# Gated attention and two expert layers on one core: routing with one division, the first second-stage expert's splits and slot loads elsewhere, the last rows by tile

## The chip, the cores and the metric

The kernel runs on one core of a Trainium2 chip. The metric is the device time of one execution in microseconds (us). The core has a matmul engine (TensorE, PE in the profile, with its weight loads as PEld), VectorE (DVE), ScalarE (ACT), GpSimd (POOL) and SyncE (SP), which only issues DMAs here. Each engine runs its own list of instructions in order, and they meet at semaphores.

## What is computed

The input is 16 sequences of 128 tokens with 256 features. Four residual blocks follow each other: attention with 16 heads over a context, a soft mixture of eight experts with silu gates, attention with one head, and a switch layer in which each token goes to one of eight experts that has 256 places. The parts that the change touches:

```python
def _routing_weights(x, Wr, temperature):                 # block 2
    inh = sigmoid(x @ Wr / temperature)
    in_zone = (inh >= GOLDEN_LOWER) & (inh <= GOLDEN_UPPER)
    dist = abs(inh - GOLDEN_CENTER)
    w = exp(-dist / 0.1) * in_zone
    no_expert = w.sum(-1, keepdims=True) < 1e-08
    fb = exp(-dist / 0.3)
    fb_w = fb * (one_hot(top_k(fb, 2)).sum(-2))
    fb_w = fb_w / clip(fb_w.sum(-1, keepdims=True), 1e-08)
    w = where(no_expert, fb_w, w)
    return w / clip(w.sum(-1, keepdims=True), 1e-08)

# block 4: di = the tokens of each expert, in the order of their places
h = relu(einsum('ecm,emh->ech', di, w1)); eo = einsum('ech,ehm->ecm', h, w2)
out = x + tanh(g_ffn[1]) * (gate of the token * its row of eo)
```

## The kernel before

Float32 products are made of three matmuls: each operand is split into a high part (a rounded copy) and a low part (the value less the copy), and high*high, high*low and low*high are summed in PSUM. So each weight matrix that is loaded needs a high half, which ScalarE writes, and a low half, a subtraction by VectorE or GpSimd.

*First stage.* A loop written out in Python goes over the 16 sequences (`b`), with attention of one sequence and the eight experts (`gate_up`, `down`) of an earlier group of four sequences between its pieces. The routing weights of a group are made by VectorE at four places: `zones`, `two_best` and `expert_weights` (L1138) in the step after the group's last sequence, for groups 0 to 2, and once more after the loop for group 3. Each routing instruction goes through `seq`, which waits for it before the next. `expert_weights` writes `w_exp`, and `accumulate` (L1070) behind it adds the first expert's result with it to `x_all`. TensorE's next `down` half waits for that on the semaphore `ac`, as PSUM has one bank for both halves.

*Second attention.* From about 550 us on, `turn3(ga, gb)` runs on each engine: it finishes group `gb` and begins group `ga`. The last call is `turn3(None, 3)`. In it VectorE normalises the rows (`root_b`, whose steps are L262 to L267, and `normalise_b`), makes the low half of their transposes (`xb_low`), and after TensorE's gate logits picks the expert and the place of each token (`pick_expert`, `count_experts`, `pick_place`). GpSimd then sends the group's rows to their places in a buffer `slots` in HBM with four indirect DMAs (`dispatch`, L2224). ScalarE's list in that turn: `probs_copy`, `split(0, 0, 0)` (the high half of the first expert's w1, L746), `xb_high` (L787), `logits1_copy`, `gate_exp`; `split(0, 0, 1)` for w2 comes behind the turn. The low half of w1 is `split_w1(0, 0)` on GpSimd (L2214), between the dispatches of groups 2 and 3; that of w2 is `split_w2(0, 0)` on VectorE (L1541), behind the turn.

*Second stage.* When all rows are dispatched, SyncE loads slots (`xs`, one row of 260 floats for each of 2048 places, 16 tiles) and the next expert's weights (`load4`). An expert takes half a turn: `slots_norm` (VectorE, L1531), `slots_transposed` (TensorE), high and low half of the transposes, eight `hidden` blocks in four PSUM banks (TensorE L1591, ScalarE's `relu` L880, VectorE's low half L1545), `down4` (TensorE L2097), `rows_out` (VectorE L1553 and L1556: row numbers, then one update for each of the two tiles) and `scatter` (GpSimd L2245: two indirect DMAs to the output). The next expert's slots and weight halves are made in the same half-turn. Three turns of two experts run in a loop on the device, the fourth is written out. `alone` is a `sem_inc` between waits.

Of the kernel before, what the change touches and what calls it, by code (L numbers as in the profile page):

```python
# [8 lines left out]
ALU = mybir.AluOpType  # L9
# [7 lines left out]
P = 128  # L17
# [81 lines left out]
def block_kernel(nc, x, ctxT, maskf, mask0, gx, gf, wa0, bcols, bv0, bo0, w0, wrs, temp, wa1, bv1,  # L99
                 w1, w2, const, out, slots, kept):  # L100
    with ExitStack() as ctx:
# [235 lines left out]
        s_xs = [sem("first_slots_loaded"), sem("other_slots_loaded")]  # L337
# [10 lines left out]
        s_sc = [sem(f"rows_scattered{i}") for i in range(2)]  # L348
        ds4 = Steps(sem("vector_step4"), 2)
# [51 lines left out]
        def _(sp):  # L401
# [132 lines left out]
            for n, tiles in enumerate((slice(0, 4), slice(4, B))):  # L534
                sp.dma_start(xs[:, tiles, :], slots[tiles.start * P:tiles.stop * P, :].rearrange("(t p) c -> p t c", p=P)
                             ).then_inc(s_xs[n], 16)
                if n == 0:
                    load4(1, slice(1, 2))
# [12 lines left out]
        def _(act):  # L551
# [294 lines left out]
            def turn3(ga, gb):  # L846

                probs_copy(gb)
                if ga is None:
                    act.wait_ge(a1, 2 * G)  # L850
                    split(0, 0, 0)
                else:
                    xa_high(ga)
                    k1_evict(ga)
                    q1_evict(ga)
# [37 lines left out]
            split(0, 0, 1)  # L893
# [6 lines left out]
        def _(dve):  # L900
# [201 lines left out]
            def divide_by_sum(i):  # L1102
                seq(dve.tensor_reduce(rs[2], r[i], AX.X, ALU.add))
                seq(dve.tensor_scalar(rs[2], rs[2], 1e-8, None, ALU.max))
                seq(dve.reciprocal(rs[2], rs[2]))
                seq(dve.tensor_tensor(r[i], r[i], over_e(rs[2]), ALU.mult))

# [30 lines left out]
            def expert_weights(g):  # L1138
                divide_by_sum(7)
                seq(dve.tensor_tensor(r[7], r[7], over_e(rs[1]), ALU.mult))  # L1140
                seq(dve.tensor_tensor(rt[4], rt[4], rt[7], ALU.add))
                divide_by_sum(4)
                if g >= 2:
                    dve.wait_ge(ac, 2 * E * (g - 1))
                dve.tensor_scalar(w_exp[g % 2], r[4], tgate[:, 2:3], None, ALU.mult).then_inc(s_wexp, 1)
# [349 lines left out]

            def turn3(ga, gb):
# [11 lines left out]
                if ga is not None:  # L1508
                    mask_and_max(ga)
# [13 lines left out]
            for s in (xd_ok, di_lo, w4_l2, h1_lo, y4, ds4, idx4):  # L1523
                s.credit(dve)

# [22 lines left out]
            def rows_out(g, i):  # L1548
                dve.wait_ge(d4.sem, d4.now(g, i + 1))
# [4 lines left out]
                for j in range(2):  # L1554
                    row = xs[:, t + j, :] if isinstance(g, int) else xs[:, bass.ds(t + j, 1), :].rearrange("p a c -> p (a c)")
                    ins = dve.scalar_tensor_tensor(yo[i][j], ps[:, 4 + i, j * D:(j + 1) * D], row[:, D + 2:D + 3],  # L1556
# [3 lines left out]
            def turn(g, last):  # L1560
                for i in range(2):
                    nxt = (g, 1) if i == 0 else (g + 1, 0)
                    more = i == 0 or not last
                    if more:
                        if i == 1:
                            dve.wait_ge(s_xs[1], 16)
                        slots_norm(*nxt)
                    for f in range(8):
                        hidden_low(g, i, f)
                    if more:  # L1570
                        slots_low(*nxt)
                        split_w2(*nxt)
                    rows_out(g, i)
            split_w2(0, 0)
# [8 lines left out]
        def _(pe):  # L1583
# [504 lines left out]
            def down4(g, i):  # L2088
                pe.wait_ge(w4_hi.sem, w4_hi.now(g, 2 * i + 2))
                pe.wait_ge(w4_l2.sem, w4_l2.now(g, i + 1))  # L2090
                pe.wait_ge(y4.sem, y4.before(g, i + 1))
                for j in range(2):
                    for f in range(8):
                        if j == 0:
                            pe.wait_ge(h1_lo.sem, h1_lo.now(g, 8 * i + f + 1))
                        for n, (a, b) in enumerate(THREE):
                            mm = pe.matmul(ps[:, 4 + i, j * D:(j + 1) * D], h4[i][a][:, f, j * P:(j + 1) * P],  # L2097
                                           w4[i][b][:, 1, f * D:(f + 1) * D], start=(f == 0 and n == 0), stop=(f == 7 and n == 2))
                mm.then_inc(d4.sem, 1)

            def turn(g, last):
                for i in range(2):
# [4 lines left out]
                    down4(g, i)  # L2107
# [6 lines left out]
        def _(pool):  # L2114
# [119 lines left out]
            split_w1(0, 0)  # L2234
# [3 lines left out]
            def scatter(g, i):  # L2238
                pool.wait_ge(y4.sem, y4.now(g, i + 1))
                pool.wait_ge(ds4.sem, ds4.now(g, i + 1))  # L2240
                pool.wait_ge(idx4.sem, idx4.now(g, i + 1))
                alone(pool)
                for j in range(2):

# [65 lines left out]
```

## Time and profile before

| | |
|---|---|
| median of 3 runs | 763.89 us (762.23 to 765.86) |
| profiled execution | 764.7 us |
| its span, first to last instruction | 762.9 us |
| mean granted TensorE clock | 0.921 |
| busy: PE / DVE / ACT / POOL | 646.4 / 521.0 / 331.2 / 229.1 us |
| first stage | to about 562 us |
| second attention | about 562 to 638 us |
| dispatch and load of the slots | about 638 to 650 us |
| second stage | about 650 to 762.9 us |

All views come from the profiled execution, and their times count from the start of its span. A line names the start, the duration, the engine, the source line, the operation, output and inputs with their shapes, and how many like instructions it merges. What stands in brackets is the time in which the engine sat idle just before, and what ended it. Matmul ends are modelled.

### The profile page before, as it was taken

Reading aid. Unit: us, or ns where it says so; the run is one execution under the profiler, and the core shown is the slowest. Engines: PE = TensorE matmul, PEld = TensorE weight load, DVE = VectorE, ACT = ScalarE, POOL = GpSimd, SP = SyncE. Lnnn points to the kernel's source line nnn. Section 1 sums busy time; section 2 is a strip of 40 time slices with the busy share of each in tenths; the row PEclk is TensorE's granted clock in tenths of the full one; section 3 lists DMA queues with packets and bytes.
Section 4 is the critical chain, followed back from the end, with each engine's and each line's share of the span. In section 5 each row is a group of like instructions: output and inputs, shape, how many; then the busy total and the mean of one; then the engine's idle time right before and its main releaser. Section 6 shows DMA issues by size and latency. Waiting matters only on the chain.

```text
span 762.9 us, 12648 instructions
## 1 busy us (share of the span) xinstructions
PE 646.4 (85%) x4564; PEld 546.7 (72%) x4564; DVE 521.0 (68%) x1362; ACT 331.2 (43%) x530; POOL 229.1 (30%) x155
## 2 busy tenths in 40 slices
PE   5978598899899899999799889999966931799995
PEld 4656366787678778778688777898855821799995
DVE  6877987677877866866776647479458883466662
ACT  4434155355356456456355325152523321455641
POOL 2444624566532212221014010010031242255542
PEclk9879779899999999999999999999989955799998
DMA  7303303335442242333243424434221141964700
GB/s 225 121 15 127 125 1 139 125 135 211 180 166 83 85 165 84 137 113 125 83 165 113 162 87 152 132 124 146 83 69 43 61 161 43 318 210 153 242 20 26
DMA packets 43463, 94.51 MB, mean 124 GB/s; under 512 B 3519, under 2 KB 24383, under 8 KB 42384
## 3 DMA queue, kind: packets, MB, share of 16 engines
q1 hardware_dynamic: 41344, 87.62, 33.6%
q0 software_dynamic: 2064, 6.16, 2.3%
q8 instruction: 33, 0.54, 0.3%
q14 instruction: 22, 0.18, 0.1%
HBM read 72.94 MB, written 21.04 MB: 123 GB/s over the span
## 4 chain that ended last, share of the span: by engine, by line
PE 65%; DVE 24%; issue 5%; ACT 2%; DMA 1%; POOL 1%; DVEq 0%; SPq 0%; ACTq 0%; POOLq 0%
PE psum L1591 43%; PE psum L2097 6%; PE psum L1668 2%; PE psum L1698 2%; PE psum L1628 2%; PE psum L1662 2%; DVE work L1063 1%; DVE scratch L266 1%; DVE x_all L1079 1%; PE psum L1635 1%; PE psum L1647 1%; DVE work L951 1%; PE psum L1962 1%; PE psum L1893 1%; PE psum L1945 1%
## 5 line engine op out<-in xcount | busy, mean ns | idle before, releaser
L1591 PE MATMUL psum<-arena 128*128 128x256 f32 (+1 forms) x2544 | 446.0, 334 | 33.8 <-DVE x_all L1079 15.6
L1591 PEld LDWEIGHTS psum<-arena 128*128 128x128 f32 x2544 | 384.5, 199 | 78.4 <-DVE x_all L1079 14.8
L2135 POOL TENSOR_TENSOR diag<-neg_ident,work 128x1024 fp32r<-128x1024 f32 x32 | 60.9, 1904 | 249.3 <-DVE work L1010 242.5
L1063 DVE TENSOR_TENSOR work<-work,psum 128x512 f32<-128x512 f32 x64 | 43.9, 686 | 62.1 <-PE psum L1591 57.3
L625 ACT ACTIVATE arena<-work 128x512 fp32r<-128x512 f32 x64 | 40.3, 630 | 90.7 <-DVE work L1063 78.7
L1079 DVE SCALAR_TENSOR_TENSOR x_all<-psum,w_exp,x_all 128x256 f32<-128x256 f32 x128 | 55.9, 479 | 27.7 <-PE psum L1591 26.9
L618 ACT ACTIVATE work<-psum 128x512 f32<-128x512 f32 x64 | 38.2, 597 | 56.8 <-PE psum L1591 56.3
L1068 DVE TENSOR_TENSOR arena<-work,arena 128x512 fp32r<-128x512 f32 x64 | 51.8, 810 | 8.7 <-ACT arena L625 8.2
L2218 POOL TENSOR_TENSOR arena<-work,arena 128x1024 fp32r<-128x1024 f32 x4 | 9.5, 2370 | 151.1 <-ACT arena L641 151.1
L1010 DVE TENSOR_REDUCE work<-psum 128x8 f32<-128x1024 f32 x32 | 39.0, 1220 | 15.7 <-PE psum L1647 15.6
L593 ACT ACTIVATE work<-psum 128x1024 f32<-128x1024 f32 x32 | 32.8, 1026 | 35.4 <-PE psum L1668 32.3
L2097 PE MATMUL psum<-arena 128*128 128x256 f32 x384 | 47.9, 284 | 0.0
L2097 PEld LDWEIGHTS psum<-arena 128*128 128x128 f32 x384 | 46.6, 192 | 0.0
L2214 POOL TENSOR_TENSOR arena<-work,arena 128x2048 fp32r<-128x2048 f32 x8 | 37.0, 4621 | 15.9 <-ACT arena L746 15.9
L880 ACT ACTIVATE arena<-psum 128x256 fp32r<-128x256 f32 x64 | 22.6, 385 | 44.1 <-PE psum L1591 43.5
L1545 DVE SCALAR_TENSOR_TENSOR arena<-psum,arena 128x256 fp32r<-128x256 f32 x64 | 24.9, 421 | 20.2 <-ACT arena L880 19.0
L618 ACT ACT_TABLE_LOAD x26 | 33.4, 1283 | 0.5
L746 ACT ACTIVATE arena<-work 128x2048 fp32r<-128x2048 f32 x16 | 30.5, 1907 | 5.1 <-DMA work<-in_w 5.1
L1662 PE MATMUL psum<-arena 32*128 32x256 f32 x384 | 32.6, 303 | 0.2 <-DVE arena L1003 0.2
L2245 POOL DMA_INDIRECT out<-work,out_idx x16 | 15.8, 990 | 51.0 <-DVE work L1556 48.5
L2224 POOL DMA_INDIRECT slots<-x_all,tok_idx x16 | 16.8, 1048 | 42.4 <-DVE tok_idx L1418 38.7
L1662 PEld LDWEIGHTS psum<-arena 32*128 32x128 f32 x384 | 25.9, 192 | 0.8 <-issue 0.8
(194 smaller groups left out, 844.8 us busy)
## 6 DMA issues: line engine op xcount, KB each, us to landing
arena<-kept SPq DMA_DIRECT2D x24, 1024.0 KB, 5.6
work<-in_w SPq DMA_DIRECT2D x16, 1024.0 KB
kept<-arena SPq DMA_DIRECT2D x8, 1536.0 KB, 6.1
arena<-kept SPq DMA_DIRECT2D x24, 512.0 KB, 4.8
work<-in_w SPq DMA_DIRECT2D x8, 768.0 KB, 7.8
slots<-fill POOLq DMA_DIRECT2D x1, 2080.0 KB
work<-in_ctxT SPq DMA_DIRECT2D x8, 256.0 KB, 3.0
work<-in_ctxT SPq DMA_DIRECT2D x4, 512.0 KB, 5.2
```

The source lines that it names most:

```text
L593: act.activation(probs[u % 2], ps[:, ST:ST + 2, :].rearrange("p j (h q) -> p (j h) q", q=P), ACT.Exp, scale=DH ** -0.5).then_inc(ex, 1)
L618: act.activation(gu[i % 2], ps[:, GA, :], ACT.Silu).then_inc(sl, 1)
L625: act.activation(hT[n % 2][0][:, m, :], gu[i % 2], ACT.Copy).then_inc(hh, 1)
L1010: dve.tensor_reduce(mx[u % 2], ps[:, MX:MX + 2, :].rearrange("p j (h k) -> p (j h) k", k=P), AX.X, ALU.max).then_inc(mx_ok, 1)
L1063: dve.tensor_tensor(gu[i % 2], gu[i % 2], ps[:, UP, :], ALU.mult).then_inc(hm, 1)
L1068: dve.tensor_tensor(hT[n % 2][1][:, m, :], gu[i % 2], hT[n % 2][0][:, m, :], ALU.subtract).then_inc(hl, 1)
L1079: ins = dve.scalar_tensor_tensor(x_all[:, g * GB + t, 0:D], ps[:, DN, j * D:(j + 1) * D], w_exp[g % 2][:, t, e:e + 1], x_all[:, g * GB + t ...
L1591: mm = pe.matmul(dst, left(i, k), right(j, k), start=(n == 0), stop=(n == 3 * K2 - 1))
L1662: pe.matmul(ps[:, ST + j, m * 256:(m + 1) * 256], kT[h % 2][i][r:r + 32, m, t:t + P], qM[h % 2][jj][r:r + 32, m, :, t:t + P], start=False, ...
L2097: mm = pe.matmul(ps[:, 4 + i, j * D:(j + 1) * D], h4[i][a][:, f, j * P:(j + 1) * P], w4[i][b][:, 1, f * D:(f + 1) * D], start=(f == 0 and ...
L2135: pool.tensor_tensor(diag, neg_ident[:, :].rearrange("p (o q) -> p o q", o=1).to_broadcast([P, 8, P]), mx[u % 2].rearrange("p (h o) -> p h ...
L2214: pool.tensor_tensor(w4[i][1][:, 0, :], raw4[i][:, 0, :], w4[i][0][:, 0, :], ALU.subtract).then_inc(w4_l1.sem, 1)
```

## The change

One division in the routing: the two best experts' weights are no longer divided by their own sum before they are chosen, the clips at 1e-8 go, and the last division becomes a factor in the instruction that writes `w_exp`. ScalarE makes both high halves of the first second-stage expert within the last attention turn. The w1 low half moves from GpSimd to VectorE, between `xb_low` and `pick_expert`; the w2 low half moves behind a wait for all dispatches. The first load of slots is cut into two of two tiles. In the second stage `slots_norm` moves from ahead of the eight low halves to behind the fourth. In the very last half-turn TensorE signals after the first tile and writes the second tile into bank 4, and VectorE updates tile by tile. In every half-turn GpSimd sends each tile once its own update is there.

```diff
-            s_xs = [sem("first_slots_loaded"), sem("other_slots_loaded")]
+            s_xs = [sem(f"{n}_slots_loaded") for n in ("first", "second", "other")]
+            d4_first = sem("last_out_first_tile_ready")
@@ SyncE
-            for n, tiles in enumerate((slice(0, 4), slice(4, B))):
+            for n, tiles in enumerate((slice(0, 2), slice(2, 4), slice(4, B))):
                 sp.dma_start(xs[:, tiles, :], slots[...]).then_inc(s_xs[n], 16)
-                if n == 0:
+                if n == 1:
                     load4(1, slice(1, 2))
@@ ScalarE, turn3
                 if ga is None:
                     act.wait_ge(a1, 2 * G)
                     split(0, 0, 0)
+                    split(0, 0, 1)
...
-            split(0, 0, 1)
             slots_high(0, 0)
@@ VectorE, routing
             def expert_weights(g):
-                divide_by_sum(7)
                 seq(dve.tensor_tensor(r[7], r[7], over_e(rs[1]), ALU.mult))
                 seq(dve.tensor_tensor(rt[4], rt[4], rt[7], ALU.add))
-                divide_by_sum(4)
+                seq(dve.tensor_reduce(rs[2], r[4], AX.X, ALU.add))
+                seq(dve.reciprocal(rs[2], rs[2]))
                 if g >= 2:
                     dve.wait_ge(ac, 2 * E * (g - 1))
-                dve.tensor_scalar(w_exp[g % 2], r[4], tgate[:, 2:3], None, ALU.mult).then_inc(s_wexp, 1)
+                dve.scalar_tensor_tensor(w_exp[g % 2], r[4], tgate[:, 2:3], over_e(rs[2]), ALU.mult, ALU.mult
+                                         ).then_inc(s_wexp, 1)
@@ VectorE, turn3
+            def first_split(a, done):
+                dve.wait_ge(w4_hi.sem, w4_hi.now(0, a + 1))
+                dve.tensor_tensor(w4[0][1][:, a, :], raw4[0][:, a, :], w4[0][0][:, a, :], ALU.subtract).then_inc(done, 1)
...
                 xb_low(gb)
-                if ga is not None:
+                if ga is None:
+                    first_split(0, w4_l1.sem)
+                else:
                     mask_and_max(ga)
...
+            dve.wait_ge(s_disp, 16 * B + 16)
+            first_split(1, w4_l2.sem)
@@ VectorE, second stage
-            def rows_out(g, i):
-                dve.wait_ge(d4.sem, d4.now(g, i + 1))
+            def rows_out(g, i, last):
+                if last:
+                    dve.wait_ge(d4_first, 1)
+                else:
+                    dve.wait_ge(d4.sem, d4.now(g, i + 1))
...
                 for j in range(2):
+                    if last and j:
+                        dve.wait_ge(d4.sem, d4.now(g, i + 1))
-                    ins = dve.scalar_tensor_tensor(yo[i][j], ps[:, 4 + i, j * D:(j + 1) * D], row[:, D + 2:D + 3],
+                    ins = dve.scalar_tensor_tensor(yo[i][j], ps[:, 4 if last and j else 4 + i, j * D:(j + 1) * D], row[:, D + 2:D + 3],
                                                    row[:, 0:D], ALU.mult, ALU.add)
...
-                    if more:
-                        if i == 1:
-                            dve.wait_ge(s_xs[1], 16)
-                        slots_norm(*nxt)
                     for f in range(8):
                         hidden_low(g, i, f)
+                        if more and f == 3:
+                            dve.wait_ge(s_xs[1 + i], 16)
+                            slots_norm(*nxt)
...
-            split_w2(0, 0)
@@ TensorE
-            def down4(g, i):
+            def down4(g, i, last):
...
+                if last:
+                    pe.wait_ge(y4.sem, y4.now(g, 1))
                 for j in range(2):
+                    bank = 4 if last and j else 4 + i
...
+                    if last and j == 0:
+                        mm.then_inc(d4_first, 1)
@@ GpSimd
-            split_w1(0, 0)
             dispatch(G - 1)
...
             def scatter(g, i):
-                pool.wait_ge(y4.sem, y4.now(g, i + 1))
-                pool.wait_ge(ds4.sem, ds4.now(g, i + 1))
                 pool.wait_ge(idx4.sem, idx4.now(g, i + 1))
                 alone(pool)
-                for j in range(2):
+                for j, rows in enumerate((ds4, y4)):
+                    pool.wait_ge(rows.sem, rows.now(g, i + 1))
+                    alone(pool)
                     pool.indirect_dma_start(...)
```

## Rows read from the trace of the kernel before

**Rows 1.** Page, chain that ended last: share of the span by engine.
```profile
PE 65%; DVE 24%; issue 5%; ACT 2%; DMA 1%; POOL 1%; DVEq 0%; SPq 0%; ACTq 0%; POOLq 0%
```

**Rows 2.** Timeline (start us, us, engine, line, operation, idle before), routing of group 0.
```profile
132.78 0.18 DVE L1103 TENSOR_REDUCE work<-work 128x4 f32<-128x32 f32 x1
...
133.64 0.19 DVE L1140 TENSOR_TENSOR work<-work 128x32 f32<-128x32 f32 x1
...
134.31 0.17 DVE L1104 TENSOR_SCALAR work<-work 128x4 f32<-128x4 f32 x1
...
134.73 0.19 DVE L1106 TENSOR_TENSOR work<-work 128x32 f32<-128x32 f32 x1
134.95 0.24 DVE L1145 TENSOR_SCALAR w_exp<-work,tgate 128x32 f32<-128x32 f32 x1
...
136.24 5.99 PE L1591 MATMUL psum<-arena 128*128 128x256 f32 x31 [2.88 <-DVE x_all L1079]
```

**Rows 3.** Timeline, TensorE behind the routing of group 1.
```profile
258.26 5.07 PE L1591 MATMUL psum<-arena 128*128 128x256 f32 x38 [2.59 <-DVE x_all L1079]
```

**Rows 4.** Timeline, last attention turn.
```profile
618.51 1.91 ACT L746 ACTIVATE arena<-work 128x2048 fp32r<-128x2048 f32 x1 [5.13 <-DMA work<-in_w]
...
620.51 4.49 POOL L2214 TENSOR_TENSOR arena<-work,arena 128x2048 fp32r<-128x2048 f32 x1 [1.51 <-ACT arena L746]
620.63 4.38 DVE L266 SCALAR_TENSOR_TENSOR scratch<-scratch,work 128x4 f32<-128x4 f32 x1
...
625.45 0.16 DVE L266 SCALAR_TENSOR_TENSOR scratch<-scratch,work 128x4 f32<-128x4 f32 x1
...
628.05 0.60 ACT L787 ACTIVATE arena<-psum 128x512 fp32r<-128x512 f32 x1 [7.63 <-PE psum L1893]
...
634.53 0.19 DVE L1390 TENSOR_REDUCE work<-psum 128x4 f32<-128x32 f32 x1 [4.30 <-PE psum L1980]
```

**Rows 5.** Timeline, dispatch of the last group.
```profile
638.77 2.29 DVE L1541 TENSOR_TENSOR arena<-work,arena 128x2048 fp32r<-128x2048 f32 x1 [0.55 <-issue]
639.79 2.11 POOL L2224 DMA_INDIRECT slots<-x_all,tok_idx  x1 [0.30 <-issue]
642.21 0.97 POOL L2224 DMA_INDIRECT slots<-x_all,tok_idx  x1 [0.30 <-issue]
```

**Rows 6.** Timeline, first slots; last, the 256 KB context loads (KB, us to landing).
```profile
646.11 0.37 SPq L535 DMA_DIRECT2D x_all<-slots  x1
...
649.89 0.74 DVE L1531 TENSOR_SCALAR work<-x_all 128x256 f32<-128x256 f32 x2 [8.83 <-DMA x_all<-slots]
...
656.84 1.90 ACT L746 ACTIVATE arena<-work 128x2048 fp32r<-128x2048 f32 x1
...
work<-in_ctxT SPq DMA_DIRECT2D x8, 256.0 KB, 3.0
```

**Rows 7.** Timeline, end of the kernel.
```profile
748.08 5.92 PE L2097 MATMUL psum<-arena 128*128 128x256 f32 x48
...
754.12 0.87 DVE L1556 SCALAR_TENSOR_TENSOR work<-psum,x_all 128x256 f32<-128x256 f32 x2
755.89 0.98 POOL L2245 DMA_INDIRECT out<-work,out_idx  x1 [9.23 <-DVE work L1556]
757.17 0.98 POOL L2245 DMA_INDIRECT out<-work,out_idx  x1 [0.30 <-issue]
```

**Rows 8.** Timeline, second expert's hidden blocks in the second stage.
```profile
672.43 1.42 DVE L1545 SCALAR_TENSOR_TENSOR arena<-psum,arena 128x256 fp32r<-128x256 f32 x4 [1.34 <-ACT arena L880]
672.90 1.49 PEld L1591 LDWEIGHTS psum<-arena 128*128 128x128 f32 x12 [0.33 <-DVE arena L1545]
...
674.34 0.46 PEld L2074 LDWEIGHTS psum<-cst,work 128*128 128x128 f32 x4
```

**Rows 9.** Windows: stretch, its length, busy us (count) by engine, PEclk, DMA share, GB/s.
```profile
134.00:140.60 6.60, 4.36 (x20) 4.36 (x21) 4.83 (x13) 0.63 (x1) 3.12 (x3) 0.50 0.00 0
...
478.90:482.10 3.20, 3.20 (x17) 3.20 (x17) 0.88 (x3) 0.56 (x1) 0.00 (x0) 0.50 0.00 0
650.70:659.30 8.60, 6.80 (x30) 6.40 (x31) 2.44 (x6) 3.62 (x6) 0.47 (x1) 0.50 1.08 363
```

More of the change, by code:

```diff
@@ L1100, in first_of_max @@
                 seq(dve.tensor_tensor(dst, dst, over_e(rs[3]), ALU.is_equal))
[L1102 to L1106, printed above, removed]
             def routing_z(g):
@@ L1572, in turn @@
                         split_w2(*nxt)
-                    rows_out(g, i)
-            split_w2(0, 0)
+                    rows_out(g, i, last and i == 1)
             dve.wait_ge(s_xs[0], 16)
@@ L2096, in down4 @@
                         for n, (a, b) in enumerate(THREE):
-                            mm = pe.matmul(ps[:, 4 + i, j * D:(j + 1) * D], h4[i][a][:, f, j * P:(j + 1) * P],
+                            mm = pe.matmul(ps[:, bank, j * D:(j + 1) * D], h4[i][a][:, f, j * P:(j + 1) * P],
                                            w4[i][b][:, 1, f * D:(f + 1) * D], start=(f == 0 and n == 0), stop=(f == 7 and n == 2))
+                    if last and j == 0:
+                        mm.then_inc(d4_first, 1)
                 mm.then_inc(d4.sem, 1)
@@ L2106, in turn @@
                         slots_transposed(*((g, 1) if i == 0 else (g + 1, 0)))
-                    down4(g, i)
+                    down4(g, i, last and i == 1)
             slots_transposed(0, 0)
```

## The prediction

> **What bounds the kernel now.** I read the chain of waits first. By its shares [rows 1] the chain is two thirds TensorE and one quarter VectorE, and the DMAs have 1%. So a VectorE step is worth something only where TensorE stands still for it, and the timeline has to say where that is. Around the edits there are five such places. (a) In each of the four routing groups TensorE stands 2.59 to 2.88 us until VectorE has written `w_exp` and accumulated one half [rows 2, 3]. (b) In the last attention turn one tiny VectorE instruction takes 4.38 us while GpSimd subtracts a weight half, and everything waits for it [rows 4]. (c) Then GpSimd's four row dispatches are the chain, and the second takes 2.11 us instead of 0.98 [rows 5]. (d) The first slots come from HBM [rows 6]. (e) After the last matmul come two row updates, two indirect DMAs and a landing [rows 7]. In between, the second-stage loop runs TensorE nearly full [rows 8].
>
> **The change, part by part.** The sum is made against the profiled execution, 764.7 us (span 762.9, 1.8 around it), which is 0.8 above the median of the three runs.
>
> *Routing.* The sequence from L1103 to L1145 is strictly serial: each instruction waits for the one before. Removed are the first four (132.78 to 133.64: 0.86), the second clip (0.17 plus the gap of 0.03: 0.20) and the second product (134.73 to 134.95: 0.22), together 1.28 [rows 2]. The last instruction becomes one with a second tensor input. The old one takes 0.24, a product with a broadcast column 0.19 [rows 2]; the trace has no such form with both, so its price lies between 0 and 0.1 more; I take 0.02, since both inputs are small. Net 1.26 per group. VectorE is what TensorE waits for in all four, and the shortest of the four waits is 2.59 [rows 3], over twice the saving, so nothing else becomes late there. Four groups: 5.0 us. The other end is that some of it is given back: afterwards VectorE and GpSimd again collide at other phases. The trace has such collisions (L266 below is the longest); a loss of half, 2.5 us, is my lower end.
>
> *First expert's splits, w1 part.* The 4.38 us of L266 run from 620.63 to 625.01, and GpSimd's L2214 from 620.51 to 625.00; the same form takes 0.16 right after [rows 4]. The change takes L2214 off GpSimd, so 4.38 - 0.16 = 4.22 us go. What is late next: ScalarE now does both high halves in a row. The weights land at 618.51, two splits of 1.91 end at 622.33, and the activation behind them (L787) will be wanted at 628.05 - 4.22 = 623.83 [rows 4], so 1.5 us of cover remain; if the weights came later than that, it would cost the excess one for one. VectorE takes over the w1 subtraction (2.29 us, the length of L1541 [rows 5]) after `xb_low`, where it sits idle 4.30 us until the gate's logits are transposed [rows 4]: hidden, with 2.0 us to spare. GpSimd's queue loses its only work between the two last dispatches. Value 4.2, bounds 2.7 and 4.2.
>
> *w2 part.* L1541 runs now from 638.77 to 641.06, and the dispatch that starts in its middle ends at 641.90, 2.11 long where its neighbours take 0.97 [rows 5]. After the change VectorE waits for all dispatches before it subtracts, so 1.13 us go. Behind that wait in VectorE's queue stand only `slots_norm` and what follows it, which need the later load anyway. The subtraction now runs in the wait for the slots: 2.29 us plus 0.05, in a wait of 3.78 (646.11 to 649.89 [rows 6]), hidden by 1.4 us. The Trainium skill speaks against this gain: in "SBUF — State Buffer", section "Who interferes with whom", a VectorE `tensor_tensor` is said not to stall a GpSimd DMA, as it takes only the read interface of the shared pair. By that rule the 2.11 would have another cause and stay, and the sum would be 1.1 less; the row's overlap speaks for the lock.
>
> *Slots in a smaller first load.* The first load has two tiles, 260 KB, instead of four, 520 KB. 520 KB take 3.78 us from issue to use; 256 KB loads take 3.0 at the median [rows 6]. I take 0.8. The ends are 0 (the load is all latency) and 1.4 (then the 2.34 of the subtraction is late next). The other side: SyncE issues one more load (0.37) ahead of the second expert's weights, and TensorE starts 0.8 sooner, so those weights have 1.2 less time. ScalarE takes them up at 656.84 without idling [rows 6]; and TensorE would need their first consumer's followers only later, since its first four column blocks run at half rate [rows 9]. I cost it at 0, up to 1 us if that cover is gone.
>
> *`slots_norm` in the middle of the eight low halves.* At the start of a half-turn TensorE waits 0.33 us for the third low half, and that one waits for ScalarE, whose weight split stands before it in ScalarE's queue [rows 8]. VectorE is free earlier but idles 1.34 us for the same split, so nothing is won. In its new place the 0.73 us fall behind the fourth low half, when VectorE is catching up; by my reckoning it ends near 673.9 against 674.34, when TensorE wants the transposes [rows 8]. Price 0; with the cover gone up to 0.7 in each of seven half-turns, some 3 us in practice.
>
> *Last rows by tile.* The 48 matmuls take 5.92 us [rows 7], so the first tile is ready 2.9 us earlier, and its index copy, update and DMA (some 0.6, 0.9 of lead, 0.98) are done near 753.7, before the last matmul. Behind the last matmul remain one update (0.45 less than 0.87 for two, and the index copy lay ahead of them as well), the lead from VectorE's end to the DMA (754.99 to 755.89, 0.90) and one DMA; the second DMA's 0.30 + 0.98 go. That is 0.45 + 1.28 = 1.7 us; the lead could shrink to the 0.30 seen between two DMAs, then 2.3. The landing of 4.75 us (758.15 to 762.9) stays. TensorE's extra wait on `y4` is for the update of the expert before, whose values VectorE takes up as soon as that expert's last matmul is done, a whole set of hidden blocks earlier. In the loop GpSimd gets one more wait, off the chain.
>
> **Sum**: 5.0 + 4.2 + 1.1 + 0.8 + 1.7 = 12.9 (12.8 by the unrounded terms). 764.7 - 12.9 = 751.8, and less the 0.8 by which the profiled run lies above the median: **751.0 us**.
>
> **Rivals.**
> *The clock helps too.* TensorE runs at half rate (1.2 GHz of 2.4) from 134.0 to 140.6 and from 478.9 to 482.1, each around a stand for routing, and for 8.6 us at the start of the second stage [rows 9]. The second of them came after an idle stretch of 2.83; this becomes 1.57. If it goes away, the 3.2 us of work at half rate take 1.6, and shorter idling ahead of the second stage may give 1 us more: 748.4. Against: in groups two and three the idle time is the same and no drop follows, so the idle time alone doesn't decide, and the shifted work can also meet new drops.
> *The routing gain is partly given back* in the long first stage, by collisions or by a new half-rate stretch (each costs 1.6 to 2.2): 751 + 2.5 = 753.5.
> *The long L266 isn't GpSimd's doing*, or the weights' landing takes its place, and the long dispatch stays: 751 + 4.2 + 1.1 = 756.3. The overlap to 0.1 us speaks against it.
> *Only the dispatch stays long*: 752.1.
> *`slots_norm` is in TensorE's way*: 754.
> *Slower.* After the pause for the dispatch TensorE is granted full clock only at 659.3. If in the changed kernel it isn't granted within the first expert, each further half-turn of 96 matmuls costs 11.8 us more (48 in 5.92). From 12.9 us on, a bit over one half-turn, the gain is gone; two give 751 + 23.6 = 774.6. Every later half-turn in the trace is at full clock and as dense, so this is unlikely.
>
> **Chances.** Forecast 0.50, clock helps 0.18, partly given back 0.18, L266 stays 0.05, dispatch stays 0.04, `slots_norm` 0.03, slower 0.02. From the helped clock to the partly lost gain with the bounds of the unknown costs around them: 746.5 to 755.5. A measurement of this kernel can tell about 0.5% (3.8 us) from no change; only "slower" and a sum of several mishaps are not below 760.1: faster 0.96, same 0.02, slower 0.02.
>
> **What would show it.** Right: TensorE's idle time before the accumulated half is near 1.6 in the first group and 1.3 in the second; no L266-type instruction over 0.2 us in the last attention turn and TensorE's transposes 4.2 us earlier; four dispatches of 0.97; first slots used about 3.0 us after their issue; the second-stage half-turns at 12.3 us as before; one DMA behind the last matmul. Wrong: ScalarE's L787 waiting for a weight split, VectorE's w1 subtraction running into the gate's pick, a new TensorE wait for the slots in the loop, or more half-rate time than before.

## The result, and the profile after

The changed kernel takes 777.47 us (median, 775.08 to 778.08) where the kernel before, on the same chip, takes 763.06. The ratio is 1.019, with a 95% interval of 1.0132 to 1.0247: slower by 14 us, where 751.0 was predicted. The profiled execution took 777.27 us, its span is 775.5 (762.9 before) and the mean granted clock 0.930 (0.921 before). So the mean clock over the whole is no worse. It doesn't say what the clock did in the one stage that got slower; that comes below.

The chain of the page, by engine, answers to [rows 1]:

```profile
PE 62%; DVE 23%; issue 9%; ACT 3%; DMA 2%; POOL 1%; DVEq 0%; SPq 0%; ACTq 0%; POOLq 0%
```

TensorE's and VectorE's shares fell, and "issue" rose from 5 to 9%: time in which an engine waits for nothing that the profile shows. That names no culprit, so I cut both timelines at four marks that exist in both: the start of the first write of `w_exp`, that of the fourth, the first hidden block, and the end of the last matmul.

| stretch, us | before | after | after less before |
|---|---|---|---|
| to the first `w_exp` | 135.0 | 130.0 | -5.0 |
| to the fourth `w_exp` | 342.3 | 335.8 | -6.5 |
| to the first hidden block | 176.3 | 170.1 | -6.2 |
| to the end of the last matmul | 100.4 | 132.4 | +32.0 |
| to the end of the span | 8.9 | 7.2 | -1.7 |

Four stretches are shorter, and one, the second stage, is a third longer. The timeline of one half-turn shows why (start, duration, engine, line, operation, the idle time before and what ended it):

```profile
658.38 4.57 POOL L2230 TENSOR_TENSOR arena<-work,arena 128x2048 fp32r<-128x2048 f32 x1
...
658.84 4.59 DVE L1538 TENSOR_SCALAR work<-x_all 128x256 f32 x2
...
663.57 1.11 PE L2084 MATMUL psum<-cst,work 128*128 128x128 f32 x4 [3.23 <-DVE work L1538]
664.33 7.12 PE L2111 MATMUL psum<-arena 128*128 128x256 f32 x48
```

L1538 is `slots_norm` in its new place. Its two instructions take 4.59 us, where the first pair, with GpSimd idle, took 0.73. They end at 663.43, which is 0.48 after GpSimd's w1 subtraction (L2230) of the next expert (658.38 + 4.57 = 662.95): the first of the pair ends within 0.1 of GpSimd's, and the second takes its own 0.4 behind it. TensorE stands 3.23 us for the transposes (L2084), which need those rows. The next pass shows the same: GpSimd from 675.49, `slots_norm` from 676.09 for 4.44, and TensorE's wait 3.06. The groups of the page, and TensorE's waits from 636 to 769 us (in total, times, longest):

```profile
L1538 DVE TENSOR_SCALAR work<-x_all 128x256 f32 (+1 forms) x16 | 31.8, 2026 | 0.5 <-DMA x_all<-slots 0.5
```

```profile
PE psum L2084 <- DVE work L1538: 21.4, 7, 3.2
```

A mean of 2026 ns for an instruction of 400 is the sign to look for: one of each pair is held. The 21.4 us of waits are seven half-turns of about 3.1. Most of the rest of the 32.0 is the clock. Windows across that same half-turn (stretch, length, then busy us and count for PE, PEld, DVE, ACT and POOL, granted clock, DMA share, GB/s):

```profile
660.50:663.50 3.00, 0.00 (x0) 0.00 (x0) 3.00 (x3) 0.26 (x1) 2.45 (x1) 1.00 0.21 69
663.50:667.00 3.50, 3.43 (x17) 3.44 (x18) 1.95 (x5) 2.20 (x2) 0.00 (x0) 0.51 0.00 0
667.00:671.00 4.00, 4.00 (x36) 4.00 (x35) 2.29 (x1) 0.19 (x1) 0.00 (x0) 1.00 0.14 11
```

TensorE idles 3 us at full clock and is then granted half of it (1.2 GHz) for about 3.5 us. Hence the transposes take 1.11 us (0.60 where the clock stays full, e4 below) and the down matmuls 7.12 (6.00 in the same place before). This happens in six of the seven half-turns that wait. In the first, with a wait of 2.75, the clock stays full, and the down matmuls take 5.99. The half-turn from 671.29 to 688.37 takes 17.08 us, where before it takes 12.34 (668.30 to 680.64): 3.63 us up to the start of the down matmuls (3.06 of wait, 0.51 in the transposes), and 1.11 in them. Six such half-turns are some 4.75 longer each, the first 3.4 (18.10 less 14.70), and the eighth, which has no `slots_norm`, is unchanged: 28.5 + 3.4 = 31.9 of the 32.0. Of the first half-turn's 3.4 some 0.8 belongs to another part of the change, the smaller first load of slots: with `slots_norm` back in its old place that half-turn takes 15.49 (e1), with four tiles loaded first as well 14.70 (e10).

The rest of the profile moved as foreseen. Routing and the last attention turn, answering to [rows 2, 3] and [rows 4, 5]:

```profile
131.32 6.86 PE L1601 MATMUL psum<-arena 128*128 128x256 f32 x40 [1.60 <-DVE x_all L1080]
...
249.95 7.34 PE L1601 MATMUL psum<-arena 128*128 128x256 f32 x48 [1.33 <-DVE x_all L1080]
...
605.67 3.71 ACT L747 ACTIVATE arena<-work 128x2048 fp32r<-128x2048 f32 x2 [3.77 <-PE psum L1972]
...
609.04 0.16 DVE L266 SCALAR_TENSOR_TENSOR scratch<-scratch,work 128x4 f32<-128x4 f32 x1
...
612.24 0.60 ACT L788 ACTIVATE arena<-psum 128x512 fp32r<-128x512 f32 x1 [2.85 <-PE psum L1903]
...
618.72 0.19 DVE L1389 TENSOR_REDUCE work<-psum 128x4 f32<-128x32 f32 x1 [2.11 <-PE psum L1990]
...
623.97 0.97 POOL L2240 DMA_INDIRECT slots<-x_all,tok_idx  x1 [0.30 <-issue]
```

TensorE's waits behind routing are 1.60 and 1.33. L266 takes 0.16, the w1 subtraction (L1497) lies inside the wait for the gate with 2.11 to spare, ScalarE had 2.85 us between the second split and the activation behind it, and all four dispatches take 0.97. The first slots, answering to [rows 6]:

```profile
629.35 0.88 SPq L536 DMA_DIRECT2D x_all<-slots  x2
...
632.20 0.73 DVE L1538 TENSOR_SCALAR work<-x_all 128x256 f32<-128x256 f32 x2 [0.55 <-DMA x_all<-slots]
...
640.65 1.91 ACT L747 ACTIVATE arena<-work 128x2048 fp32r<-128x2048 f32 x1 [1.36 <-DMA work<-in_w]
```

From issue to use the slots take 2.85 us (3.78 before). But ScalarE now waits 1.36 for the second expert's weights, where before it waited for nothing. The end, answering to [rows 7]:

```profile
762.41 5.92 PE L2111 MATMUL psum<-arena 128*128 128x256 f32 x48
...
768.37 0.48 DVE L1568 SCALAR_TENSOR_TENSOR work<-psum,x_all 128x256 f32<-128x256 f32 x1 [2.32 <-PE psum L2111]
769.73 0.98 POOL L2259 DMA_INDIRECT out<-work,out_idx  x1 [1.83 <-DVE work L1568]
```

One update and one DMA stand behind the last matmul, and from its end to the span's end it is 7.2 us instead of 8.9.

### The profile page after: what moved, and what is told of

It reads as the page before. It is cut to its first block, busy times and chain, and to the rows that moved or that the text cites. A ratio compares the mean times of both kernels' runs of the same rounds, so it can differ in the third digit from the quotient of the medians.

```text
span 775.5 us, 12635 instructions
## 1 busy us (share of the span) xinstructions
PE 648.7 (84%) x4564; PEld 550.0 (71%) x4564; DVE 539.8 (70%) x1339; ACT 330.8 (43%) x530; POOL 223.2 (29%) x154
## 4 chain that ended last, share of the span: by engine, by line
PE 62%; DVE 23%; issue 9%; ACT 3%; DMA 2%; POOL 1%; DVEq 0%; SPq 0%; ACTq 0%; POOLq 0%
PE psum L1601 39%; PE psum L2111 7%; PE psum L1678 2%; PE psum L1708 2%; PE psum L1672 2%; PE psum L1638 2%; DVE work L1064 1%; DVE x_all L1080 1%; PE psum L1645 1%; PE psum L1657 1%; DVE work L952 1%; DMA work<-in_w 1%; PE psum L1972 1%; PE psum L1955 1%; PE psum L1903 1%
## 5 line engine op out<-in xcount | busy, mean ns | idle before, releaser
L2111 PE MATMUL psum<-arena 128*128 128x256 f32 x384 | 54.5, 308 | 0.0
L1011 DVE TENSOR_REDUCE work<-psum 128x8 f32<-128x1024 f32 x32 | 39.0, 1219 | 12.9 <-PE psum L1657 12.8
L1552 DVE SCALAR_TENSOR_TENSOR arena<-psum,arena 128x256 fp32r<-128x256 f32 x64 | 24.4, 416 | 20.3 <-ACT arena L882 20.3
L2084 PE MATMUL psum<-cst,work 128*128 128x128 f32 x32 | 8.4, 416 | 34.0 <-DVE work L1538 34.0
L2230 POOL TENSOR_TENSOR arena<-work,arena 128x2048 fp32r<-128x2048 f32 x7 | 31.9, 4556 | 15.2 <-ACT arena L747 15.2
L1538 DVE TENSOR_SCALAR work<-x_all 128x256 f32 (+1 forms) x16 | 31.8, 2026 | 0.5 <-DMA x_all<-slots 0.5
```

The costliest lines, as they stand in the source:

```text
L1011: dve.tensor_reduce(mx[u % 2], ps[:, MX:MX + 2, :].rearrange("p j (h k) -> p (j h) k", k=P), AX.X, ALU.max).then_inc(mx_ok, 1)
L2111: mm = pe.matmul(ps[:, bank, j * D:(j + 1) * D], h4[i][a][:, f, j * P:(j + 1) * P], w4[i][b][:, 1, f * D:(f + 1) * D], start=(f == 0 and n ...
L2230: pool.tensor_tensor(w4[i][1][:, 0, :], raw4[i][:, 0, :], w4[i][0][:, 0, :], ALU.subtract).then_inc(w4_l1.sem, 1)
```

## The experiments

The theory (T): `slots_norm` in its new place starts while GpSimd's 4.6 us subtraction runs, is held until that ends, and TensorE's wait for it brings a half-rate stretch; the loss of the second stage comes from that one move, and the other parts gain what was forecast. The rivals: (R1) it is the place itself, since VectorE is too late there for the transposes, whoever runs beside it; (R2) the smaller loads of slots, or the weights that now come later, delay each half-turn; (R3) it takes the other parts, whose earlier second stage meets other phases.

**e1: the move alone is undone.** Of the changed kernel:

```diff
-                    for f in range(8):
-                        hidden_low(g, i, f)
-                        if more and f == 3:
-                            dve.wait_ge(s_xs[1 + i], 16)
-                            slots_norm(*nxt)
+                    if more:
+                        dve.wait_ge(s_xs[1 + i], 16)
+                        slots_norm(*nxt)
+                    for f in range(8):
+                        hidden_low(g, i, f)
```

> The changed kernel with slots_norm back ahead of the eight low halves; nothing else differs. Theory (the move of slots_norm behind the fourth low half is the whole loss, and every other part of the change gains as in the sum): from TensorE's first hidden block (635.94 in the changed kernel's trace) to its last matmul there it took 132.4 us, in the kernel before 100.4 us; putting the step back gives 777.5 - 32 = 745 to 747 us, the two slots_norm instructions take 0.73 us together and half-turns 12.3 us. Rival (the loss comes from the other edits of the second stage, the per-tile waits of scatter or the split slot load): it stays above 765.

Measured: 747.39 us (743.15 to 751.73), ratio to the kernel before 0.981 (0.9743 to 0.9877). The second stage takes 101.2 us. In the groups and the timeline `slots_norm` is back at its length, and GpSimd's subtraction starts after it:

```profile
L1538 DVE TENSOR_SCALAR work<-x_all 128x256 f32 (+1 forms) x16 | 5.9, 410 | 0.6 <-DMA x_all<-slots 0.6
```

```profile
665.61 0.78 DVE L1538 TENSOR_SCALAR work<-x_all 128x256 f32 x2
...
668.29 1.42 DVE L1552 SCALAR_TENSOR_TENSOR arena<-psum,arena 128x256 fp32r<-128x256 f32 x4 [1.23 <-ACT arena L882]
668.36 4.65 POOL L2230 TENSOR_TENSOR arena<-work,arena 128x2048 fp32r<-128x2048 f32 x1
...
670.65 6.00 PE L2111 MATMUL psum<-arena 128*128 128x256 f32 x48
```

So 31.2 of the second stage's 32.0 us hang on this move (132.4 less 101.2). These rows also show what GpSimd does not hold: L1552, with one input in PSUM, takes 1.42 for four beside the subtraction, as in [rows 8]. R2 falls but for the 0.8 us that are left over 100.4, since the loads are those of the changed kernel.

**e3: the move alone is made** in the kernel before (the edit of e1 the other way round, with the semaphores of before).

> The kernel before with slots_norm alone moved behind the fourth low half. Theory: this one edit costs what the second stage lost, 3.4 us in the first half-turn and 4.8 in each of six, 32 us: 763 + 32 = 795, with slots_norm at 4.1 to 4.6 us for its two instructions. Rival (it needs the other edits beside it): 763 to 770.

Measured: 799.05 us (795.25 to 800.33), ratio 1.0466 (1.0411 to 1.0521). `slots_norm` has a mean of 2216 ns. Timeline:

```profile
674.59 4.57 POOL L2214 TENSOR_TENSOR arena<-work,arena 128x2048 fp32r<-128x2048 f32 x1
...
674.63 5.01 DVE L1531 TENSOR_SCALAR work<-x_all 128x256 f32 x2
...
679.77 1.11 PE L2074 MATMUL psum<-cst,work 128*128 128x128 f32 x4 [3.64 <-DVE work L1531]
680.53 8.30 PE L2097 MATMUL psum<-arena 128*128 128x256 f32 x48
```

By the traces this is 35.6 us more than the kernel before, and the second stage alone takes 137.8 instead of 100.4, so R3 falls too: the move costs this without any of the others. The median is 4 us above the expectation's 795, since half-turns are 17.5 to 18.8 us here. GpSimd's instruction begins some 4.7 to 5.0 us into each half-turn (4.2 to 4.3 in the changed kernel) and ends as much later, `slots_norm` starts at once with it, and TensorE waits 3.5 to 3.9. In two of the half-turns, that of the rows among them, the half-rate stretch also reaches further into the down matmuls (8.30 instead of 7.12).

**e4: the place is kept, its neighbour goes.** In the second stage VectorE makes the w1 low halves of all following experts too, behind the eight low halves; GpSimd makes none.

```diff
                     if more:
                         slots_low(*nxt)
+                        split_w1v(*nxt)     # dve.tensor_tensor(..., ALU.subtract).then_inc(w4_l1.sem, 1)
                         split_w2(*nxt)
@@ GpSimd
-                    if not last:
-                        split_w1(g + 1, i)
...
-            split_w1(0, 1)
```

> The changed kernel, slots_norm still behind the fourth low half, but the w1 subtraction of the following experts is done by VectorE ahead of its w2 subtraction, and GpSimd does none. Theory of the lock: with no subtraction on GpSimd the two slots_norm instructions take 0.73 us at the same place; VectorE gains 2.3 us of work per half-turn while TensorE is in the down projection, which it has room for, so half-turns are near 12.3 to 12.7 us and the time 745 to 750. Rival of the order: the place is unchanged, so the time stays near 777.

Measured: 749.59 us (743.64 to 751.29), ratio 0.9842 (0.9792 to 0.9891). Half-turns take 12.33. Timeline:

```profile
678.51 0.73 DVE L1538 TENSOR_SCALAR work<-x_all 128x256 f32 x2
679.15 1.08 DVE L1556 SCALAR_TENSOR_TENSOR arena<-psum,arena 128x256 fp32r<-128x256 f32 x3
...
679.84 0.60 PE L2089 MATMUL psum<-cst,work 128*128 128x128 f32 x4
...
681.80 2.28 DVE L1548 TENSOR_TENSOR arena<-work,arena 128x2048 fp32r<-128x2048 f32 x1
```

R1 falls. Behind the fourth low half `slots_norm` takes 0.73 and ends 0.60 us ahead of the transposes. The place is harmless by itself; GpSimd's work at that moment makes it costly.

**e5: the place and GpSimd's work are kept, the engine changes.** ScalarE normalises behind its fourth block.

```diff
+                        if more and f == 3:
+                            act.wait_ge(s_xs[1 + i], 16)
+                            slots_norm(*nxt)   # act.activation(xd[j], row[:, 0:D], ACT.Identity, bias=row[:, D + 1:D + 2], scale=row[:, D:D + 1])
@@ VectorE
-                        if more and f == 3:
-                            dve.wait_ge(s_xs[1 + i], 16)
-                            slots_norm(*nxt)
```

> The changed kernel, but the normalisation behind the fourth block is done by ScalarE (one activation per tile with a scale and a bias column) instead of VectorE, while GpSimd's weight subtraction goes on beside it. Theory of the lock between VectorE and GpSimd: ScalarE isn't held, each activation takes about 0.4 us (0.39 to 0.41, like others of 128x256), half-turns stay near 12.3 to 12.7 and the time is 746 to 751. Rival (GpSimd's subtraction holds back whoever reads the same memory, ScalarE too): activations over 1 us and a time above 765.

Measured: 746.23 us (742.83 to 749.37), ratio 0.9798 (0.975 to 0.9846). Timeline:

```profile
678.02 1.09 ACT L889 ACTIVATE work<-x_all 128x256 f32 x2
678.04 4.63 POOL L2238 TENSOR_TENSOR arena<-work,arena 128x2048 fp32r<-128x2048 f32 x1
...
679.91 0.60 PE L2092 MATMUL psum<-cst,work 128*128 128x128 f32 x4
```

The same work starts with GpSimd's and isn't held on ScalarE: the lock seen here is one between VectorE and GpSimd. The size was off: an activation takes 0.605 us, where some 0.4 was expected. From the second half-turn on there is room for it (12.33 to 12.34); the first takes 16.29, where it takes 15.49 in e1.

**e2 and e11: other places.** e2 puts `slots_norm` behind the second low half, ahead of GpSimd's start; e11 behind the sixth, late in GpSimd's instruction. The edit in both is one figure of the changed kernel:

```diff
-                        if more and f == 3:
+                        if more and f == 1:        # e2; in e11 f == 5
```

> The changed kernel with slots_norm behind the second low half instead of the fourth. Theory of the lock (the two instructions are held because GpSimd's weight subtraction runs at that moment, whatever their place in the list): behind the second low half VectorE idles for ScalarE's split, and GpSimd's subtraction begins only when that split has ended, so the two run unheld, 0.73 us, and the time is that of the kernel with the step ahead, 745 to 747. Rival of the order (the step in the middle of the low halves delays the low halves behind it, the later the fewer cover): the place is still in the middle, so some us per half-turn remain, 755 to 770.

> The changed kernel with slots_norm behind the sixth low half. Theory of the lock (VectorE is let go when GpSimd's subtraction ends): slots_norm starts later and takes less, some 3.3 to 3.7 us instead of 4.4 to 4.6, but ends at the same moment, so half-turns stay near 17 us and the time at 775 to 779. Rival (the pair is slowed by a fixed factor beside GpSimd): it takes 4.5 us again and ends later, half-turns near 18 us and the time above 783.

Measured: e2 747.7 us (746.63 to 750.39), ratio 0.9813 (0.9763 to 0.9863). e11 781.48 (774.96 to 783.97), ratio 1.0209 (1.0122 to 1.0295), a median 2.5 us over the expected band, with three of four runs above it. Its second stage takes 132.6 us, the changed kernel's 132.4, so the surplus doesn't come from there. Timeline of e2, then of e11:

```profile
668.59 0.89 DVE L1538 TENSOR_SCALAR work<-x_all 128x256 f32 x2
...
670.35 4.64 POOL L2230 TENSOR_TENSOR arena<-work,arena 128x2048 fp32r<-128x2048 f32 x1
```

```profile
678.65 4.55 POOL L2230 TENSOR_TENSOR arena<-work,arena 128x2048 fp32r<-128x2048 f32 x1
...
679.91 3.77 DVE L1538 TENSOR_SCALAR work<-x_all 128x256 f32 x2
...
683.81 1.11 PE L2084 MATMUL psum<-cst,work 128*128 128x128 f32 x4 [3.06 <-DVE work L1538]
```

In e11 `slots_norm` starts 1.26 us after GpSimd instead of some 0.5, and takes 3.77 instead of 4.5: it is let go when GpSimd ends (678.65 + 4.55 = 683.20, then one instruction to 683.68). So it is a lock with a fixed end and not an instruction slowed by a factor; and a start 0.5 or 1.26 us into GpSimd's instruction costs TensorE the same 3.1 us. That is what the Trainium skill says in "SBUF — State Buffer", section "Who interferes with whom", of VectorE's instructions in a two-port mode, `tensor_scalar` among those that can enter one: the one issued first keeps the shared ports for its whole length, and the other "fully blocks". The traces agree in all three kernels where `slots_norm` starts beside GpSimd's subtraction (the changed one, e3 and e11).

**e6, e7 and e8: the other parts alone** on the kernel before: e6 only the routing, e7 only the first expert's splits (both halves on VectorE, w2 behind the dispatches, both high halves in ScalarE's last turn), e8 only the last rows by tile. Their edits are those parts of the change's diff.

> The kernel before with the routing of the changed kernel alone. By the prediction's term 1.26 us per group, 5.0 in all, near 756.5 for 761.4 before; TensorE's wait for the accumulated half falls from 2.88 to 1.6 in the first group and from 2.59 to 1.3 in the second. Rival (partly given back by later collisions): 758 to 761.

> The kernel before with the first second-stage expert's splits of the changed kernel alone. By the prediction 4.2 (no L266 over 0.2 us in the last attention turn) and 1.1 (four dispatches of 0.97), 5.3 in all: near 756. Rival (the wait for the weights or for the slots takes its place): 759 to 761.

> The kernel before with the last rows by tile alone, and the per-tile waits of scatter. By the prediction the stretch from the last matmul's end to the end of the span falls from 8.9 to 7.2 us: 1.7 us, near 759.7, close to what the spread of the runs can hide; the trace decides.

| part | forecast gain | measured gain | median | ratio to before |
|---|---|---|---|---|
| e6 routing | 5.0 | 7.8 | 754.99 | 0.9901 (0.9872 to 0.9931) |
| e7 first splits | 5.3 | 6.9 | 755.85 | 0.993 (0.9903 to 0.9958) |
| e8 last rows | 1.7 | 2.2 | 760.64 | 0.9968 (0.9942 to 0.9994) |

The measured gain is the difference of the medians, to 762.8 for the kernel before. The intervals are some 2 us wide on each side, so e7 (5.3 by its ratio) and e8 agree with their forecasts; e6's interval (5.3 to 9.8 us) begins just above its 5.0. In e7 all four dispatches take 0.97; in e8 the stretch behind the last matmul is 7.15 us (8.9 before). For the rest of e6, windows of the kernel before, then of e6:

```profile
470.00:484.00 14.00, 11.17 (x68) 10.18 (x67) 9.07 (x29) 2.86 (x6) 0.00 (x0) 0.88 0.29 89
```

```profile
466.00:480.00 14.00, 12.81 (x82) 11.33 (x81) 8.88 (x21) 2.10 (x4) 0.00 (x0) 1.00 0.39 145
```

From the first `w_exp` to the fourth e6 takes 337.0 us where the kernel before takes 342.3. That is 5.3 for three groups that were to bring 3.8, and it goes with the routing edit: the nine kernels that have it take 335.2 to 337.2 us for this stretch, the four that don't (before, e3, e7, e8) 342.2 to 345.7.

Whether the clock is behind the surplus is another question, and the traces leave it open. The half-rate stretch of [rows 9] at 478.9 isn't there in e6: the window around it has a mean granted clock of 0.88 before, and e6, whose fourth `w_exp` is 8.2 us earlier (469.1 for 477.3), has the full clock around that. Nor does it have the one at 205.7 to 209.1 (0.86 in 200 to 212 before, 1.00 in e6). But the first of these lies behind the fourth `w_exp`, and the one that was at 451.6 to 454.8 before is longer in e6, 441.5 to 448.2 (0.50 in both windows). Neither do the two that vanish follow the edit: e3, with the routing of before, has the full clock from 201 to 213 and from 477 to 492, and e2 and e4, with the new one, have half of it at 202.0 to 205.2 and 197.4 to 200.4. No run varied TensorE's waits by themselves.

**e9: is it the subtraction that holds the dispatch?** e1 without the wait for the dispatches ahead of the w2 subtraction:

```diff
-            dve.wait_ge(s_disp, 16 * B + 16)
             first_split(1, w4_l2.sem)
```

> The changed kernel with slots_norm ahead, and VectorE's w2 subtraction no longer waiting for the dispatches, so that it runs right behind the choice of the places, beside GpSimd's dispatches. Theory (a VectorE tensor_tensor with two inputs in the same memory holds the dispatch): one of the last four dispatches takes about 2.1 us instead of 0.97, the slots' load is issued 1.1 us later. Rival (the long dispatch of the kernel before had another cause): all four take 0.97.

Measured, in two runs: 747.7 us, ratio 0.978 (0.9695 to 0.9865), which a microsecond can't be read from. The trace can show it, though:

```profile
623.07 2.29 DVE L1497 TENSOR_TENSOR arena<-work,arena 128x2048 fp32r<-128x2048 f32 x1 [0.55 <-issue]
624.07 2.13 POOL L2239 DMA_INDIRECT slots<-x_all,tok_idx  x1 [0.30 <-issue]
626.51 0.97 POOL L2239 DMA_INDIRECT slots<-x_all,tok_idx  x1 [0.30 <-issue]
```

With the subtraction beside it again, the dispatch that starts in its middle takes 2.13, and its neighbour 0.97. VectorE's instruction ends at 625.36, so the dispatch goes on 0.84 us longer (626.20). This is [rows 5] over again, while all sixteen dispatches of e1 take at most 1.07; and it contradicts the Trainium skill's statement in the section named above that a `tensor_tensor` doesn't stall a GpSimd DMA. For this form, two inputs in SBUF and 2048 elements wide, the trace decides against it.

**e10: the first load of slots with four tiles again**, on e1 (the semaphores for the loads follow it and aren't shown):

```diff
-            for n, tiles in enumerate((slice(0, 2), slice(2, 4), slice(4, B))):
+            for n, tiles in enumerate((slice(0, 4), slice(4, B))):
...
-                if n == 1:
+                if n == 0:
                     load4(1, slice(1, 2))
```

> The changed kernel with slots_norm ahead, and the first load of slots of four tiles again. By the prediction the time from that load's issue to the first slots_norm is 3.8 us instead of the 3.0 forecast (2.85 in the changed kernel's trace); ScalarE's wait for the second expert's weights, 1.36 us there, gets shorter or goes. In all 0 to 1 us slower than with two tiles, under what the runs' spread can show.

Measured, in two runs: 748.31 us, ratio 0.9788 (0.9707 to 0.9869), not to be told from e1's time. In the trace:

```profile
631.43 0.37 SPq L536 DMA_DIRECT2D x_all<-slots  x1
...
635.45 0.73 DVE L1538 TENSOR_SCALAR work<-x_all 128x256 f32<-128x256 f32 x2 [1.72 <-DMA x_all<-slots]
...
642.40 1.90 ACT L747 ACTIVATE arena<-work 128x2048 fp32r<-128x2048 f32 x1
```

With four tiles the slots take 4.02 us from issue to use, with two 2.85. But ScalarE finds the second expert's weights there, for which it waits 1.72 us in e1. From the issue to the second expert's transposes it is 16.25 us with four tiles and 15.86 with two. Of 1.2 us gained at the slots 0.4 is left; the first half-turn gives back 0.8 (15.49 us in e1, 14.70 in e10).

## Why the prediction was wrong

**The step that failed** is "`slots_norm` in the middle of the eight low halves ... Price 0; with the cover gone up to 0.7 in each of seven half-turns, some 3 us in practice". It cost 31.2 (132.4 us of second stage against e1's 101.2). The prediction asked when VectorE would be free and when TensorE would want the transposes, and both answers were good: it had `slots_norm` end 0.44 us ahead of TensorE, and e4, where GpSimd is idle, has it end 0.60 ahead. It never asked what GpSimd does at that moment. The answer was in the trace of the kernel before: in each of the seven half-turns that prepare another expert the w1 subtraction runs there for 4.6 us. In the half-turn of [rows 8], for which the prediction let `slots_norm` end near 673.9, it is this:

```profile
673.07 4.66 POOL L2214 TENSOR_TENSOR arena<-work,arena 128x2048 fp32r<-128x2048 f32 x1
```

The clash was even known: the same document took L266, held for 4.38 us by that very instruction [rows 4], as its second largest term, and read it as something that the change removes. The rule wasn't applied to the step that the change moves under the same instruction. The sign of being wrong that the prediction named, "a new TensorE wait for the slots in the loop", is what came.

**The rival "`slots_norm` is in TensorE's way: 754"** named the place, with the wrong mechanism and a tenth of the price. It bounded a held pair by the pair's own length, 0.7 us. The right bound was in [rows 4]: the length of the other engine's instruction, some 4.5, less TensorE's slack. To this comes what a wait of 3 us does to the clock, 1.6 us a pass in six of seven (0.51 in the transposes, 1.1 in the down matmuls). **The rival "slower"** had the right sign by another mechanism: it had the full clock withheld at the start of the stage, but there it is granted from 640 on, 4 us into the first half-turn. **The range** left the case out, since it put only 0.03 on any trouble from this step.

**What held**, against the sum's terms:
- *Routing, 5.0.* The waits went down to 1.60 and 1.33, exactly as said, and the new last instruction takes 0.25 against 0.24 (0.02 more reckoned). Alone the part gives 7.8 with 2.3 of uncertainty, so the term was if anything too small, and no loss to later collisions shows. Whether the rival "the clock helps too" is the reason isn't shown: two half-rate stretches vanished and another grew (e6).
- *w1 part, 4.2; w2 part, 1.1.* L266 takes 0.16, and the dispatches 0.97. ScalarE's cover was 2.85 instead of 1.5, since its first split waited for TensorE and no longer for the weights' DMA, and VectorE's 2.11 where 2.0 was reckoned. Together with the slots' load the stretch from the fourth `w_exp` to the first hidden block is 6.2 us shorter; the terms are 4.2 + 1.1 + 0.8 = 6.1. The weighing of the long dispatch, row against rule, came out for the row (e9).
- *Smaller first load, 0.8.* 0.93 at the slots themselves (3.78 to 2.85). "I cost it at 0, up to 1 us if that cover is gone": the cover for the weights was gone, and the first half-turn of e1 takes 15.49 us instead of 14.70. The net is about 0.4 (e10).
- *Last rows, 1.7.* 1.7 in the changed kernel's trace and in e8's. The lead from VectorE's end to the DMA is 0.88 (0.90 reckoned), the landing 4.8.

Without the one move (e1) the kernel takes 747.39 us: 14.0 less than the kernel before beside it, where 12.9 was the sum. So close a match is partly luck: the interval is 9.4 to 19.6 less, and the parts measured alone add up to 16.9 even without the slots' load. In the table of the first section the first 5.0 us hold one routing group, 1.3; the rest is not the change's. The kernel before was later by 3.6 already at the first instruction that the change touches, and other kernels have their first `w_exp` anywhere from 127.5 to 135.4 us.

e1, e2, e4 and e5, and e9 and e10 that build on e1, all beat both kernels. e5 has the lowest median, 746.23, but its runs (742.83 to 749.37) overlap those of the others, so which of the six is best stays open. Also open is what brings the first stage more than the shorter waits, and what makes half-rate stretches come and go there.

## What to carry to other kernels

When an instruction is moved, look at what every other engine runs at its new place, and GpSimd above all: a short VectorE scale (`slots_norm`) or tiny update (L266) whose operands lie in SBUF waited for all that was left of a long GpSimd instruction that began first, so its price is bounded by the length of that one and not by its own. Not every VectorE instruction waits so: those with an input in PSUM didn't here. A known clash is a rule for the whole kernel: after reading one as something to gain, go through all moved steps for the same pair. And price a new TensorE wait of some 3 us in a dense loop with the slower matmuls behind it, here half as much again in six cases of seven.

## What the runs showed of the hardware that was not expected

- A 128x256 `tensor_scalar` from SBUF to SBUF takes 0.40 us alone and is held for the whole rest of a GpSimd 128x2048 subtraction of 4.55: pairs of 4.59, 4.44 and 3.77 us, ending 0.5 us after GpSimd each time. VectorE's instructions with one input in PSUM ran at their usual 0.42 beside it. Nor is every one that reads only SBUF held: in the kernel before, three 128x256 `BATCH_NORM_STATS2` of x_all (L1150, from 387.66) took their usual 0.41 each while a GpSimd subtraction (L2135) ran from 386.75 to 388.65.
- A VectorE subtraction of 2.29 us with both inputs in SBUF stretched a GpSimd indirect DMA that began in its middle from 0.97 to 2.13 us.
- In the changed kernel six waits of 3.0 to 3.2 us in a dense loop were each followed by about 3.5 us at half the TensorE clock, and one of 2.75 wasn't. The half-turns before, without such waits, had the full clock from 659.7 to the last matmul, although the mean clock over the kernel was higher in the slower one (0.930 against 0.921).
- A ScalarE activation of 128x256 from SBUF with scale and bias columns takes 0.605 us (two in 1.09, which overlap a little), where one of the same size from PSUM without them takes 0.38; which of the differences costs the time, no run shows.
